# A graph network kernel on one core: the first node step inside the attention pass, parted scale chains, the first convolution's product ahead of the degrees, 16 address words

## The reference, cut to what matters

```
x = layernorm(x + D^-1/2 A D^-1/2 (x @ W))              # W 256x256, A from src, dst; D: in-degrees
for l in range(3):
    Q, K, V = per node type, per head (8 heads of 32): xh @ W_Q, W_K, W_V
    scores  = (Q[dst] . (K[src] @ W_E[edge type])) / sqrt(32) * mu[l, head, edge type]
    w       = softmax of the scores over the edges of one destination
    agg     = sum over the edges of one destination of w * V[src]
    x = layernorm(x + agg @ Wo + bo) * ln1_g + ln1_b
    x = layernorm(x + gelu(x @ w1 + b1) @ w2 + b2) * ln2_g + ln2_b
x = layernorm(x0 + layernorm(x) * out_g + out_b)        # x0: the rows that entered the three layers
```

## Time and profile before

| | us |
|---|---|
| median of three runs (lowest, highest) | 6251.01 (6250.25, 6252.13) |
| the profiled execution, and its span | 6244.92, 6243.2 |
| index_tiles | 7 to 155 |
| gcn_edges | 155 to 1189 |
| gcn_nodes | 1189 to 1379 |
| attention pass and node stage, layer 0 | 1379 to 2455, 2455 to 3042 |
| layer 1 | 3042 to 4119, 4119 to 4704 |
| layer 2 | 4704 to 5781, 5781 to 6243 |

### The profile page before, as it was taken

How to read it: one execution, slowest core, us unless ns; L and a number is a source line. 1 busy time by engine, 2 the same in 40 slices (tenths; PEclk the granted TensorE clock), 3 DMA queues, 4 the chain that set the end, 5 groups by cost and what they waited for, 6 DMA issues and landing times. The chain is left out here.

```text
span 6243.2 us, 121147 instructions
## 1 busy us (share of the span) xinstructions
PE 5319.2 (85%) x27435; PEld 4193.2 (67%) x27436; DVE 4546.4 (73%) x10942; ACT 2877.7 (46%) x8789; POOL 3893.5 (62%) x3826
## 2 busy tenths in 40 slices
PE   5777777788888888999788888889997888888997
PEld 4444444576666666889666666678895666666886
DVE  6433333658888897665588898866647888888797
ACT  3555555554555554223355555532243555555343
POOL 1777777657777774335577777733356777776343
PEclk8888788899999999999899999999998999999998
DMA  3554444578888884105888888821188888887111
GB/s 124 169 158 146 145 147 143 179 254 263 250 252 251 249 249 146 34 30 174 271 251 252 248 250 251 251 73 32 34 261 263 251 250 249 249 251 212 38 50 39
DMA packets 568568, 1153.46 MB, mean 185 GB/s; under 512 B 86570, under 2 KB 327788, under 8 KB 568412
## 3 DMA queue, kind: packets, MB, share of 16 engines
q0 software_dynamic: 239984, 774.78, 42.1%
q1 hardware_dynamic: 303743, 353.43, 17.2%
q10 hardware_dynamic: 24684, 23.58, 1.2%
HBM read 960.31 MB, written 191.18 MB: 184 GB/s over the span
## 5 line engine op out<-in xcount | busy, mean ns | idle before, releaser
L1843 POOL DMA_INDIRECT at_kv<-kv_table,idx_kv x1664 | 1578.6, 949 | 551.3 <-issue 454.8
L1859 ACT COPY sums<-ps x2499 | 949.7, 380 | 1499.3 <-PE ps L1976 1481.1
L1940 PE MATMUL ps<-at_wv,at_hot 128*128 128x264 f32 x3328 | 1039.4, 429 | 170.9 <-ACT at_hot L1871 63.7
L803 POOL DMA_INDIRECT gc_rows<-x_scaled,idx_x x832 | 792.4, 952 | 340.2 <-issue 244.6
L1843 POOL DMA_INDIRECT at_kv_last<-kv_table,idx_kv x832 | 790.3, 950 | 272.0 <-issue 216.7
L1976 PE MATMUL ps<-sums,at_hot_t 128*128 x3328 | 883.7, 389 | 25.9 <-DVE at_prod L2030 20.0
L996 PE MATMUL ps<-gc_rows,gc_hot 128*128 128x256 f32 x1664 | 664.9, 523 | 213.7 <-DMA gc_rows<-x_scaled,idx_x 212.1
L1940 PEld LDWEIGHTS ps<-at_wv,at_hot 128*128 128x128 f32 x3328 | 503.8, 191 | 402.5 <-DVE at_wv L2048 151.3
L1976 PEld LDWEIGHTS ps<-sums,at_hot_t 128*128 128x128 f32 x3328 | 618.4, 194 | 125.2 <-ACT at_hot_t L1894 25.6
L2030 DVE TENSOR_TENSOR at_prod<-ps,at_kv 128x512 f32<-128x512 f32 x832 | 572.1, 688 | 153.8 <-DMA at_kv<-kv_table,idx_kv 124.5
L2048 DVE TENSOR_TENSOR at_wv<-ps,at_kv 128x528 f32<-128x528 f32 x832 | 580.5, 698 | 98.6 <-ACT ps L1903 97.0
(11 more groups left out here) (424 smaller groups left out, 10204.5 us busy)
## 6 DMA issues: line engine op xcount, KB each, us to landing
kv_table<-pj_v_next SPq DMA_DIRECT2D x98, 396.0 KB, 3.5
kv_table<-pj_k_next SPq DMA_DIRECT2D x98, 384.0 KB, 2.8
at_hot_t<-hot_columns SPq DMA_DIRECT2D x104, 256.0 KB
at_kv<-kv_table,idx_kv POOLq DMA_INDIRECT x1664, 3.7
at_hot<-hot_rows SPq DMA_DIRECT2D x104, 256.0 KB, 4.9
at_rec<-block_records SPq DMA_DIRECT2D x104, 226.0 KB, 3.8
kv_table<-gc_rows SPq DMA_DIRECT2D x49, 396.0 KB, 3.2
kv_table<-gc_rows SPq DMA_DIRECT2D x49, 384.0 KB, 2.6
```

Of the source, the lines that this page charges most:

```text
L803: nc.gpsimd.indirect_dma_start(g.gcn_rows[:, (2 * k + j) * D:(2 * k + j + 1) * D], None, g.xs_d, bass.IndirectOffsetOnAxis(index, 0)).then ...
L1843: nc.gpsimd.indirect_dma_start(kv[:, 2 * k + j, :], None, g.tab_d.rearrange("t n c -> (t n) c"), bass.IndirectOffsetOnAxis(index, 0)).then ...
L1859: act.copy(dest, source).then_inc(evacuated, 1)
L1940: mm = t.matmul(own[j], hot[:, slot % HRING, j, :], wv[:, slot % WRING, j, :], start=False, stop=True, skip_group_check=True)
```

## The change

It has four parts.

- **The first node step in the pass.** In the turn TURNS of each pass the engines do step 0 of the node stage (windows 0 and 1) beside the drain, in four ring slots that are free by then (class FirstStep): SP loads x, POOL adds bo, DVE averages at k = 5, PE transposes at k = 6, ACT copies at k = 7, PE multiplies by Wo at k = 8, DVE adds and measures at k = 9, computes the scales at k = 10 and norms at k = 12, POOL adds b2. The node stage's step 0 only moves semaphores on then. The next projection's weights are turned in step 0 and mixed in step 1. Eleven semaphores more are cleared at the end of a node stage.
- **16 address words.** At k = 4, 8 and 12 of that turn PE reads 16 words, not 24 (its query products are over).
- **Parted scale chains.** In gcn_nodes a batch's scales are computed in four parts, one each in the four steps that follow, between the step's `keys` and its `prepare`.
- **The convolution's product ahead of the degrees.** PE no longer waits for base_ready; 6 windows go ahead of the matmul L408 that spreads the window ends, 8 ahead of that of the window numbers, 18 before the places, 9 before the counts, 8 after dis. ACT scales windows 25 to 40 by dis. The x loads 2 to 4 (ten windows each) are issued by ACT after its windows 1, 3 and 5 rather than all at the start.

```diff
-        EARLY, MIDDLE, BY_ACT = 24, 32, 25
+        FIRST, SECOND, EARLY, MIDDLE, BY_ACT = 6, 14, 32, 41, 25
...
-                t.wait_ge(end_ready, 1)
-                t.matmul(ps[:, 0, END_AT], g.ones[:], end_diag[:], start=True, stop=True).then_inc(end_spread, 1)
...
-                t.wait_ge(base_ready, 1)
                 t.wait_ge(w_in, 16)
-                transform(0, 8)
+                transform(0, FIRST)
+                t.wait_ge(end_ready, 1)
+                t.matmul(ps[:, 0, END_AT], g.ones[:], end_diag[:], start=True, stop=True).then_inc(end_spread, 1)
+                transform(FIRST, SECOND)
                 t.wait_ge(wdiag_ready, 1)
                 for c in range(CHUNKS):
                     mm = t.matmul(ps[:, 4 + c // 4, (c % 4) * P:(c % 4 + 1) * P], g.ones[:], wdiag[:, c, :], start=True, stop=True)
                 mm.then_inc(wrow_spread, 1)
-                transform(8, EARLY)
+                transform(SECOND, EARLY)
...
-                for k, (w0, w1) in enumerate(LOADS):
+                def load_x(k):
+                    w0, w1 = LOADS[k]
                     act.dma_start(x_rows[:, w0:w1, :], g.x[w0 * P:w1 * P, :].rearrange("(w p) c -> p w c", p=P)).then_inc(x_in[k], 16)
-                    if k == 0:
-                        act.dma_start(w_gcn[:], g.gcn_w.rearrange("(c k) n -> k c n", c=2)).then_inc(w_in, 16)
-                act.dma_start(x_rows[0:N - whole * P, whole, :], g.x[whole * P:N, :]).then_inc(x_in[-1], 16)
+                    if k == len(LOADS) - 1:
+                        act.dma_start(x_rows[0:N - whole * P, whole, :], g.x[whole * P:N, :]).then_inc(x_in[k], 16)
+                load_x(0)
+                act.dma_start(w_gcn[:], g.gcn_w.rearrange("(c k) n -> k c n", c=2)).then_inc(w_in, 16)
+                load_x(1)
...
+                        if w % 2 == 1 and 2 + w // 2 < len(LOADS):
+                            load_x(2 + w // 2)
...
+                transform(FIRST, SECOND)
+                transform(SECOND, EARLY)
...
+            if apart:
+                return
...
+    def scales_in_parts(self, v, k):
+        m, part, par = self.m, slice(0, len(GCN_LISTS[k])), k % 2
+        value, root, bits, half = m.var[:, part], m.rstd[:, par, part], m.bits[:, part], m.half[:, part]
+        def then(inst):
+            self.signals += 1
+            inst.then_inc(self.vec, 1)
+            v.wait_ge(self.vec, self.signals)
+        for win in range(part.start, part.stop):
+            d = v.bn_aggr(m.mom[:, win, :], m.stat[:, win:win + 1, :])
+        then(d)
+        then(v.tensor_scalar(value, m.mom[:, part, 1], EPS, None, ALU.add))
+        then(v.tensor_single_scalar(bits, value.bitcast(I32), 1, ALU.arith_shift_right))
+        then(v.tensor_scalar(root.bitcast(I32), bits, -1.0, float(SEED), ALU.mult, ALU.add))
+        yield
+        for again in range(3):
+            then(v.tensor_tensor(half, value, root, ALU.mult))
+            then(v.scalar_tensor_tensor(out=half, in0=half, scalar=-0.5, in1=root, op0=ALU.mult, op1=ALU.mult))
+            then(v.scalar_tensor_tensor(out=root, in0=half, scalar=1.5, in1=root, op0=ALU.add, op1=ALU.mult))
+            if again < 2:
+                yield
+        v.scalar_tensor_tensor(out=m.shift[:, par, part], in0=m.mom[:, part, 0], scalar=-1.0, in1=root,
+                               op0=ALU.mult, op1=ALU.mult).then_inc(self.scales_ready, 1)
+        yield
...
-            done = GCN_STARTS[GCN_IN_PASS]
+            done, parts, left = GCN_STARTS[GCN_IN_PASS], None, 0
             for n in range(-1, FILLED):
                 if n >= 0:
                     pj.keys(v, n)
+                if parts:
+                    next(parts)
+                    left -= 1
+                    parts = parts if left else None
                 for win in range(done, gcn_prepared(n)):
-                    gn.prepare(v, win)
+                    gn.prepare(v, win, apart=True)
                     done = win + 1
+                    if done in GCN_STARTS:
+                        assert not parts
+                        parts, left = gn.scales_in_parts(v, gcn_batch(win)), SCALE_PARTS
...
+        fs = FirstStep(kv, (PAIRS - RING) % RING)
+        freed = PAIRS - RING + fs.FREED
+        final_block = READY_BY // TILES + 1
+        AVERAGE_AT, TURN_AT, COPY_AT, ATTEND_AT, ADD_AT, SCALE_AT, FIRST_AT = 5, 6, 7, 8, 9, 10, 12
...
+                sp.wait_ge(weighed, freed)
+                sp.dma_start(fs.x, g.x_d[bass.ds(NPAD * layer, 2 * P), :].rearrange("(a p) c -> p a c", a=2)).then_inc(nw.x_in, 16)
...
+                pool.wait_ge(nw.loaded, 16 * 10)
+                pool.wait_ge(nw.x_in, 16)
+                nc.gpsimd.tensor_tensor(fs.x, fs.x, both(nw.rows[:, BO]), ALU.add).then_inc(nw.biased, 1)
+                pool.wait_ge(nw.x1_ready, 1)
+                nc.gpsimd.tensor_tensor(nw.x1b_first[:], nw.x1_first[:], both(nw.rows[:, B2]), ALU.add).then_inc(nw.x1_biased, 1)
...
+                    if ending and k == COPY_AT:
+                        act.wait_ge(nw.turned, 1)
+                        act.copy(fs.at.rearrange("p w c n -> p (w c n)"), ps[:, 0, :]).then_inc(nw.copied, 1)
...
-                        words[:] = block_words(32, PE_ENGINE, i, k, PE_TOPS)
+                        if isinstance(i, int) and i == TURNS and k > 0:
+                            at_sums = 4 * WORDS * i + (k // LOT_DUOS) * WORDS + LOT
+                            words[:] = [None] * LOT + load_words(nc, g.tab[32:33], PE_ENGINE, at_sums, PE_TOPS[LOT:])
+                        else:
+                            words[:] = block_words(32, PE_ENGINE, i, k, PE_TOPS)
...
+                    if isinstance(i, int) and i == TURNS and k == TURN_AT:
+                        t.wait_ge(nw.averaged, 1)
+                        t.wait_ge(multiplied, PAIRS)
+                        for q in range(4):
+                            tr = t.transpose(ps[:, 0, q * P:(q + 1) * P], fs.a[:, q // 2, (q % 2) * P:(q % 2 + 1) * P], g.ident[:])
+                        tr.then_inc(nw.turned, 1)
+                    if isinstance(i, int) and i == TURNS and k == ATTEND_AT:
+                        t.wait_ge(nw.loaded, 16 * 10)
+                        t.wait_ge(nw.copied, 1)
+                        for w in range(2):
+                            for c in range(2):
+                                mm = t.matmul(ps[:, 1, w * D:(w + 1) * D], fs.at[:, w, c, :], nw.wo[:, c, :], start=c == 0, stop=c == 1)
+                        mm.then_inc(nw.attended, 1)
...
+                def first_step(k):
+                    if k == AVERAGE_AT:
+                        sums = g.sums[:, UROW:3 * UROW].rearrange("p (w h e) -> p w h e", w=2, h=HEADS)
+                        v.wait_ge(weighed, freed)
+                        v.wait_ge(merged, final_block)
+                        v.wait_ge(evacuated, TILES * final_block + 1)
+                        v.tensor_scalar(fs.some, sums[:, :, :, HD], SOFT_EPS, None, ALU.add).then_inc(nw.shared, 1)
+                        v.wait_ge(nw.shared, 1)
+                        v.reciprocal(fs.part, fs.some).then_inc(nw.shared, 1)
+                        v.wait_ge(nw.shared, 2)
+                        v.tensor_tensor(fs.a.rearrange("p w (h e) -> p w h e", h=HEADS), sums[:, :, :, 0:HD],
+                                        fs.part[:, :, :, None].to_broadcast([P, 2, HEADS, HD]), ALU.mult).then_inc(nw.averaged, 1)
+                    if k == ADD_AT:
+                        v.wait_ge(nw.loaded, 16 * 10)
+                        v.wait_ge(nw.attended, 1)
+                        v.wait_ge(nw.biased, 1)
+                        v.tensor_tensor(fs.y, ps[:, 1, :].rearrange("p (w c) -> p w c", w=2), fs.x, ALU.add).then_inc(nw.vec, 1)
+                        v.wait_ge(nw.vec, 1)
+                        row_statistics(v, fs.y, fs, 0, nw.scaled)
+                    if k == SCALE_AT:
+                        row_scales(v, fs, range(2), nw.scaled, 0)
+                    if k == FIRST_AT:
+                        for w in range(2):
+                            d = v.scalar_tensor_tensor(out=fs.yg[:, w], in0=fs.y[:, w], scalar=fs.mom[:, w, 0:1], in1=nw.rows[:, LN1_G],
+                                                       op0=ALU.subtract, op1=ALU.mult)
+                        d.then_inc(nw.vec, 1)
+                        v.wait_ge(nw.vec, 2)
+                        for w in range(2):
+                            d = v.scalar_tensor_tensor(out=nw.x1_first[:, w], in0=fs.yg[:, w], scalar=fs.rstd[:, w:w + 1],
+                                                       in1=nw.rows[:, LN1_B], op0=ALU.mult, op1=ALU.add)
+                        d.then_inc(nw.x1_ready, 1)
...
-                    if real(n):
+                    if in_pass(n):
+                        t.nop().then_inc(a_turned, 1)
+                    elif real(n):
...
-                                tr = t.transpose(ps[:, 2, q * P:(q + 1) * P], x1[:, 1 - b, w, c * P:(c + 1) * P], g.ident[:])
```

(39 more changed lines are left out.)

51 lines of the change are left out of this document (42 added, 9 removed).

## The result

The changed kernel takes 6214.43 us (median of five runs, 6209.66 to 6222.49) against 6250.25 for the kernel before on the same chip, a ratio of 0.9946 (95% interval 0.9935 to 0.9957): 34 us less, 27 to 41. On two other chips the same kernel came to 0.9943 (0.9929 to 0.9956) and 0.9952 (0.9939 to 0.9966).

A forecast was written before the change was run, and what follows sets the result against it. No engine is full, so each phase has its own bound: POOL's gathers the convolution's pass, PE the node stages. Terms -6.8, -16 and -4.5 sum to -27.3, from 6251.0 to 6223.7 us; range 6209 to 6237.

The forecast's parts named there:

- Product ahead of the degrees: Index stage: dis 3.5 us earlier, then 3.3 gained from dis to first gather; -6.8 us, bounds -3 and -8.3.
- ninth window: Index stage, before the counts: takes PE's 1.27 us wait for DVE and no more, 1.1 to 1.3 us.
- first rival: Index stage: moved loads hold ACT, L408 comes late, product ahead gives 1 to 2 us instead of 6.8; 6229, chance 0.10.
- Parted chains: gcn_nodes: scales in parts remove most of PE's excess gaps at the scales; -16 us, bounds -21.8 and +41.
- cap of 21.8: gcn_nodes: PE's excess at the scales, 7.27 us a batch over three batches, 21.8 us at most to gain.
- 0.7 us lost in each of eight steps: gcn_nodes, batches 3 and 4: each parted step loses this to POOL's mask, 5.6 us in all.
- adding up of contended work: gcn_nodes, a parted step: about 0.7 + 0.5 us contended work against 1.16 us free of POOL's mask.
- last rival: gcn_nodes: every parted step blocked twice under a mask, for the part and for L1348; +41, 6281 us, chance 0.03.
- First node step and words: Node stages' starts gain 12.5 us, passes cost 2.5 each, clears 0.5; -4.5 us, bounds -11 to +3.
- four transposes of the finished rows: Layer 2's node stage start: 1.1 us at the lower clock level, hidden layer at about 7.9 instead of 17.46.
- all of PE's work at the lower level: Layers 0 and 1 starts: hidden layer 14.8 to 15.2 us behind the barrier, gain 1.5 each, 5 if clock is high.
- weights' gate in layers 0 and 1: Node stages' starts: next layer's weights gate PE, their turning put at 6 us behind the barrier.

The follow-up runs named there:

- third-load experiment: Changed kernel with the third load of x also issued at the start, fourth and fifth after windows 1 and 3; ratio 0.9946 to the kernel before.
- two longer parts: Changed kernel with the scale chains in two parts instead of four; 6227.07 us, ratio 0.9961 to the kernel before.
- weights experiment: Changed kernel with the next layer's projection weights turned and mixed in step 2, behind the first hidden layer; ratio 0.9942 to the kernel before.
- kernel with whole scales: Changed kernel with only the parted scale chains undone, each batch's scales in one go; 6236.14 us, ratio 0.9982 to the kernel before.

## Why the prediction was right, and where its terms were off

The time, 6214.4, lies in the range of 6209 to 6237, and the sign and order are as forecast: 27.3 us forecast, 35.8 between the medians. The range is 28 us wide; of the three terms one fell short by 2 us and two were exceeded by 3 and 8, so that the time alone says little of the working. The terms:

1. **Product ahead of the degrees: -6.8 forecast, -4.7 measured** (-5.6 at the first gather). Places at 65.80 against 65.6 worked out: right. From dis to the gather 23.7 against 23.3: right, the stores set it. Off was dis, 2.7 instead of 3.5 earlier, below the 3.1 to 5.0 that I had allowed: 0.2 of it at the places, the rest behind them, where I had counted on 0.4 less up to dis and 0.2 more passed (40.22 for 40.00), since the ninth window cost more than the wait it took. At the places two errors met, which was luck: I had let PE go on at 32.20, and it could only at 33.15, since the probe that DVE's window ends need landed later behind the moved loads; PE's 26 windows then took 32.65, not 33.4. The third-load experiment gives the earlier restart back. The first rival's mechanism thus existed, 1.1 us of it (the spread at 32.68 instead of 31.54), on the transfers, not in ACT's queue: its issues between copies cost 0.37, 0.37 and 0.72, and the last, 4.51 from 27.19, was over before PE's next window. Of the 5.6 at the first gather 0.9 was lost in the pass and behind it, which is within what passes differ by.
2. **Parted chains: -16 forecast, -19.4 measured.** The cap of 21.8 and the mechanism were right; the 0.7 us lost in each of eight steps, 5.6 in all, was mis-sized, about 2. The step that failed is the adding up of contended work: I counted part and addition as both needing the mask-free time, each with its wait. They come one behind the other, so the first waits for the mask and the other then runs free (0.48). The last rival, a second block in one step, did not occur in the rows of four parts above; two longer parts begin to show it (0.86 and 1.89 in one step).
3. **First node step and words: -4.5 forecast, -12.5 measured** (-11 with the passes' and the later steps' +1.7 and -0.3). That is outside the bounds I gave, -11 to +3; my own terms would have given wider ones, about -24 to +12. Mis-sized on both sides. The drains grew by 1.7 to 2.0, not 2.5; DVE's scales did set it, as PE's wait on the late weighings showed (0.55 us, in all three), and 0.6 to 1 us of it is the collision of POOL with DVE that I hadn't seen. The starts gave 17.95, not 12.5, and this is the term that failed. In layer 2 I added the four transposes of the finished rows, 1.1 us, to 6.7 us that held a wait of PE for ACT's copy; they run in that wait, and the product of Wo starts 3.24 us behind the barrier where it started 3.16 before. The other 0.5 is the clock, which rises about 5.8 us behind the barrier, within that product. In layers 0 and 1 I had all of PE's work at the lower level. In the first trace after, the level holds to about 10 us behind the barrier: the turning took 1.89 us, not 1.05 (which was a price at the upper level, as the earlier trace rows and the weights experiment's 1.04 show), the product of Wo 1.99, not 3.5. What decides how long the lower level lasts stays open: four of eighteen starts held it to the first hidden layer and beyond, although PE, once it had begun, worked there without a gap. Against that, the weights' gate in layers 0 and 1 was right (turning began 5.9 behind the barrier, forecast 6), and the weights experiment shows that it was the gate.

The collision in the drain follows the same rule that I had weighed for the masks. The Trainium skill, "SBUF — State Buffer", section "Who interferes with whom": a VectorE operation with two SBUF inputs and a GpSimd operation that reads SBUF shut each other out. Here 1.08 us instead of 0.19 under POOL's 1.41, and 0.19 when POOL's operation is moved; the trace agrees.

## What to carry to other kernels

When another engine's periodic operation blocks yours, what counts is how often your queue has to wait for it in one period, not how many of your operations could be blocked: short pieces that run back to back behind one wait are nearly free, and the piece must end before the next period, as the two longer parts showed. At a restart behind a barrier, ask which transfer gates the first work and whether other work can go in front of it, and whether added work fits into a wait that is there already; price the work at both clock levels, since the same start came out at 13 or at 17 us here by the level alone. Moving loads later to clear a queue can leave the DMA engines idle: look at the GB/s of the stretch.

## What the runs showed of the hardware that I had not expected

- With the first step in the drain, PE's clock falls to the lower level within some drains and not in others of the same program. In the kernel with whole scales, layer 2, by stretch:

```profile
5752.50:5759.00 6.50, 6.50 (x23) 4.66 (x24) 5.05 (x14) 1.49 (x6) 0.00 (x0) 0.50 0.00 1
...
5760.00:5770.00 10.00, 8.69 (x45) 6.16 (x45) 6.90 (x24) 6.31 (x19) 0.00 (x0) 1.00 0.00 0
```

  0.50 for 6.5 us, then 1.00; that drain took 35.69 instead of 32.6 and 32.69 in the other two layers (30.74 instead of 28.80 and 28.90 from DVE's last score product; the rest is a late last gather). Over all traces such a fall lies in 12 of the 30 drains that hold the first step with the addition of bo early, three of them among the unaltered kernel's nine, and in 1 of the 6 with it held back. None of the three drains of before, nor of the kernel with the step back in the node stage, showed it. What starts it stays open.
- At the restart the level also differs between executions of the same program. In the changed kernel's last trace, layer 0:

```profile
2441.50:2459.00 17.50, 11.82 (x44) 9.89 (x45) 3.99 (x10) 3.52 (x5) 1.26 (x1) 0.52 0.30 59
```

  0.52 over 17.5 us, and the first hidden layer at 16.63 behind the barrier instead of 13.47, 13.31: most of that layer's gain was gone in that execution. Both may be part of why the changed kernel's runs on one chip lie 8 to 13 us apart; that was not tried.
